# Building one tile's weights on ScalarE and VectorE instead of TensorE, at the start of a fused mixture-convolution and quantised feed-forward kernel

## The reference

```python
agg_w = jnp.einsum('bk,koi->boi', att, weight[..., 0])
y = jnp.einsum('boi,bih->boh', agg_w, x) + agg_b[:, :, None]
qg, sg = quant(y * inv_gate); qu, su = quant(y * inv_up)      # round(v / scale), scale = max|v| / 127
gate = (qg @ w_gate.T) * sg * s_wgate; up = (qu @ w_up.T) * su * s_wup
inter = clip(silu(gate) * up, -10, 10)
qi, si = quant(inter * inv_inter)
out = x + (qi @ w_down.T) * si * s_wdown
```

## Time and profile before

| | |
|---|---|
| median of 3 runs | 804.18 us (804.02 to 804.37) |
| profiled execution | 804.37 us, of which the span from first to last instruction is 802.6 us |
| TensorE busy | 793.7 us, 99% |
| VectorE busy | 716.2 us, 89% |
| ScalarE busy | 441.0 us, 55% |
| GpSimd busy | 146.1 us, 18% |

### The profile page before, as it was taken

The page is one execution under the profiler, slowest core; times in us unless marked ns, Lnnn a source line. Parts: engine busy times, 40 slices in busy tenths (PEclk is TensorE's granted clock), DMA queues, the critical chain, the costliest instruction groups (busy, mean ns, idle before and its releaser), DMA issues.

```text
span 802.6 us, 9187 instructions
## 1 busy us (share of the span) xinstructions
PE 793.7 (99%) x3521; PEld 365.1 (45%) x3521; DVE 716.2 (89%) x810; ACT 441.0 (55%) x385; POOL 146.1 (18%) x138
## 2 busy tenths in 40 slices
PE   8999999999999999999999999999999999999997
PEld 4554444444444444444444444444444444444443
DVE  6987899999888998888998888998888988888968
ACT  6774335556664545654555654555654546655531
POOL 2603210210122220122220222210222210222000
PEclk9999999999999999999999999999999999999999
DMA  9997745554445444445444455445455544354342
GB/s 298 241 216 154 163 135 179 146 170 124 127 145 171 145 145 123 120 151 169 146 145 118 118 158 164 150 145 111 120 163 159 156 136 128 107 168 153 94 108 105
DMA packets 162964, 119.81 MB, mean 149 GB/s; under 512 B 151780, under 2 KB 152164, under 8 KB 153703
## 3 DMA queue, kind: packets, MB, share of 16 engines
q1 hardware_dynamic: 161192, 106.64, 44.7%
q0 software_dynamic: 1728, 12.58, 7.7%
HBM read 60.48 MB, written 33.55 MB: 117 GB/s over the span
## 4 chain that ended last, share of the span: by engine, by line
PE 91%; DVE 6%; ACT 2%; issue 1%; DMA 0%; DVEq 0%; ACTq 0%
PE gate_ps L614 26%; PE up_ps L614 26%; PE down_ps L717 23%; PE conv_ps L567 12%; DVE amax L1093 1%; PE gate_ps L717 1%; ACT y L810 0%; DVE region L1165 0%; PE down_ps L572 0%; DVE down_sc L1257 0%; DVE xt L1266 0%; DVE part_max L1172 0%; PE conv_ps L572 0%; ACT wd L810 0%; DVE region L1111 0%
## 5 line engine op out<-in xcount | busy, mean ns | idle before, releaser
L717 PE MATMUL down_ps<-wd,qiT 128*128 128x512 bf16 x896 | 211.2, 379 | 0.0
L614 PE MATMUL gate_ps<-wg,qgT 128*128 128x512 bf16 x928 | 205.7, 379 | 0.0
L614 PE MATMUL up_ps<-wu,quT 128*128 128x512 bf16 x896 | 202.4, 379 | 0.0
L1093 DVE TENSOR_REDUCE amax<-region 128x1 f32<-128x2048 f32 (+1 forms) x90 | 173.1, 1923 | 1.2
L442 POOL TENSOR_TENSOR prod<-wexp,att_bc 128x1024 f32<-128x1024 f32 x28 | 53.1, 1896 | 540.2 <-DVE region L1151 498.5
L717 PEld LDWEIGHTS down_ps<-wd,qiT 128*128 128x128 bf16 x896 | 87.5, 98 | 123.4 <-issue 29.1
L614 PEld LDWEIGHTS gate_ps<-wg,qgT 128*128 128x128 bf16 x928 | 90.7, 98 | 109.5 <-issue 1.1
L614 PEld LDWEIGHTS up_ps<-wu,quT 128*128 128x128 bf16 x896 | 87.7, 98 | 106.1 <-ACT quT L886 0.4
L821 ACT ACTIVATE qg<-region,recip 128x2048 f16<-128x2048 f32 x30 | 60.1, 2002 | 128.3 <-DVE recip L1103 128.3
L567 PE MATMUL conv_ps<-xt,aggw 128*128 128x512 f32 x244 | 116.3, 599 | 1.4 <-ACT y L810 0.8
L810 ACT ACTIVATE y<-conv_ps,aggb 128x512 bf16<-128x512 f32 x116 | 78.9, 686 | 60.0 <-PE conv_ps L567 55.4
(11 more groups left out here) (180 smaller groups left out, 581.2 us busy)
## 6 DMA issues: line engine op xcount, KB each, us to landing
xt<-x SPq DMA_DIRECT2D x30, 1024.0 KB, 4.8
out<-xt SPq DMA_DIRECT2D x29, 1024.0 KB, 4.0
wg<-w_gateT POOLq DMA_DIRECT2D x4, 1024.0 KB, 20.5
wu<-w_upT POOLq DMA_DIRECT2D x4, 1024.0 KB, 17.2
wd<-w_downT POOLq DMA_DIRECT2D x4, 1024.0 KB, 8.6
xt<-x SPq DMA_DIRECT2D x4, 512.0 KB, 4.7
invg_bc<-inv_gate SPq DMA_DIRECT2D x1, 1024.0 KB, 8.7
out<-xt SPq DMA_DIRECT2D x2, 512.0 KB, 2.9
```

The costliest lines, as they stand in the source:

```text
L614: last = nc.tensor.matmul(acc[:, n * BANK:(n + 1) * BANK], codes[:, k * P:(k + 1) * P], wts[:, k, n * BANK:(n + 1) * BANK], start=(k == 0) ...
L717: last = nc.tensor.matmul(down_bank(t, c), qiT_at(t)[:, k * P:(k + 1) * P], wd[:, k, c * BANK:(c + 1) * BANK], start=(k == ks[0]), stop=(k ...
L1093: nc.vector.tensor_reduce(amax[:, i:i + 1], src, axis=AX.X, op=ALU.max, apply_absolute_value=True).then_inc(max_ready, 1)
```

## The change

Tile 2's experts are multiplied by eight ScalarE products into a free part of wu (`prod2`) and added up by three VectorE sums in place of TensorE's eight products; the division by the softmax sum moves into ScalarE's writing of y. The sums stand in VectorE's list after the second quarter of tile 0. Tile 3's diagonal blocks are made by GpSimd (L465's product, now for tile 3 and ahead of the weights), no longer by VectorE. TensorE does convolutions 0, 1 and 2 in one go, and convolution 3 where convolution 2 was. Tile 3's y has a home of its own (quT), so that it waits for less. The gate weights' transfers wait for input 1 instead of input 0, and input 3 is issued without waiting. The orders of ScalarE and VectorE are changed accordingly: VectorE does gate 1, gate 2, up 0, up 1 instead of gate 1, up 0, gate 2, up 1. GpSimd issues the up weights only when the sums are done.

```diff
-        Y_HOME = [y[:, :], wd_part(0, bf16), wd_part(1, bf16)]
+        Y_HOME = [y[:, :], wd_part(0, bf16), wd_part(1, bf16), quT[:, :]]
...
+        prod2 = wu[:, 4:6, :].rearrange("p k i -> p (k i)").bitcast(fp32).rearrange("p (k o) -> p k o", o=P)
...
-            sp.wait_ge(wg_in[0], 16)
             sp.dma_start(xslot(3), x[3, :, :]).then_inc(x_in[3], 16)
...
-            pool.wait_ge(x_in[0], 16)
+            pool.wait_ge(att_dve, BIAS[0])
+            a = att_bc[:, EARLY * K:FIRST * K].unsqueeze(2).to_broadcast([P, K, P])
+            nc.gpsimd.tensor_tensor(diag_at[EARLY].rearrange("p (k r) -> p k r", r=P),
+                                    ident[:, :].unsqueeze(1).to_broadcast([P, K, P]), a, ALU.mult).then_inc(diag_pool, 1)
+            pool.wait_ge(x_in[1], 16)
             for i in range(WCH):
                 load(wg, w_gateT, i, wg_in)
-            pool.wait_ge(exp_done, 1)
-            pool.wait_ge(agg_mm, 1)
-            a = att_bc[:, 2 * K:3 * K].unsqueeze(2).to_broadcast([P, K, P])
-            nc.gpsimd.tensor_tensor(diag_at[2]...).then_inc(diag_pool, 1)
             pool.wait_ge(rows_in[0], 16)
             spread(invu_bc[:, :], rows_s[:, 0:2 * I])
...
+            pool.wait_ge(sum2, 3)
             for i in range(WCH - 1):
                 load(wu, w_upT, i, wu_in)
...
             conv(0)
             conv(1)
-            aggregate_mm(2)
+            conv(2)
             turn_g(0, range(1))
-            aggregate_mm(3)
+            aggregate_mm(EARLY)
             gate(0, range(4))
             turn_g(0, range(1, 2))
-            conv(2)
+            conv(EARLY)
             turn_g(1)
             gate(0, range(4, 8))
             gate(1, HALVES[0])
-            conv(3)
...
+            def experts2(ks):
+                for k in ks:
+                    nc.scalar.activation(prod2[:, k, :], wexp[:, k, :], ACT.Copy, scale=att_col(2, k)).then_inc(scaled2, 1)
...
+                elif t == 2:
+                    act.wait_ge(xu_ready, FIRST)
...
-            conv_out(0)
+            experts2(range(4))
+            conv_out(0, range(1))
+            experts2(range(4, 6))
+            conv_out(0, range(1, 2))
+            experts2(range(6, 7))
+            conv_out(0, range(2, NC))
+            experts2(range(7, K))
             conv_out(1)
+            conv_out(2, range(1))
             quant_g_first(0)
-            aggregate_out(2)
+            conv_out(2, range(1, 2))
+            quant_g_first(1)
             turned_g(0, range(1))
-            quant_g_first(1)
-            aggregate_out(3)
+            aggregate_out(EARLY)
+            conv_out(2, range(2, NC))
             turned_g(0, range(1, 2))
             quant_g(1)
-            conv_out(2, range(2))
-            turned_g(1, range(1))
-            conv_out(2, range(2, NC))
-            turned_g(1, range(1, 2))
+            conv_out(EARLY)
+            turned_g(1)
+            quant_g(2)
             quant_u(0)
-            conv_out(3)
-            quant_g(2)
             turned_g(2)
...
+            def experts2_sum():
+                dve.wait_ge(scaled2, K)
+                nc.vector.tensor_tensor(prod2[:, 0:4, :], prod2[:, 0:4, :], prod2[:, 4:8, :], ALU.add).then_inc(sum2, 1)
+                dve.wait_ge(sum2, 1)
+                nc.vector.tensor_tensor(prod2[:, 0:2, :], prod2[:, 0:2, :], prod2[:, 2:4, :], ALU.add).then_inc(sum2, 1)
+                dve.wait_ge(sum2, 2)
+                nc.vector.tensor_tensor(aggw2, prod2[:, 0, :], prod2[:, 1, :], ALU.add).then_inc(sum2, 1)
...
+                    if c == 1:
+                        experts2_sum()
...
             quant_first()
-            diagonals(3)
             quant_g(1)
+            quant_g(2)
             quant_u(0)
-            quant_g(2)
             quant_u(1)
             xg_product(3)
             gate_out(0)
```

More of the change, by code:

```diff
@@ L92, in y_at @@
         def y_at(t):
-            return Y_HOME[t] if t < EARLY else y[:, :]
+            return Y_HOME[t] if t <= EARLY else y[:, :]
         def xg_at(t):
@@ L145, in adaln_ffn @@
         ones = qiT[:, 0:2 * P].bitcast(fp32)
+        aggw2 = qiT[:, 4 * P:6 * P].bitcast(fp32)
         filler = region1[:, 0:(P + BANK) // 2].bitcast(bf16)
@@ L159, in adaln_ffn @@
         SPLIT = 5
-        diag_at = [region2[:, I:H], prod_flat, region2[:, I:H], prod_flat]
+        diag_at = {0: region2[:, I:H], EARLY: region2[:, I:H]}
+        prod2 = wu[:, 4:6, :].rearrange("p k i -> p (k i)").bitcast(fp32).rearrange("p (k o) -> p k o", o=P)
         def diag_part(t, k):
@@ L245, in adaln_ffn @@
         diag_act = sem("diag_act")
-        diag_dve = sem("diag_dve")
+        scaled2 = sem("scaled2")
+        sum2 = sem("sum2")
         diag_pool = sem("diag_pool")
@@ L300, in conv_bank @@
         def conv_bank(t, c):
-            return bank(up_ps, c - 2) if t < EARLY and c >= 2 else bank(conv_ps, c % 2)
+            return bank(up_ps, c - 2) if t <= EARLY and c >= 2 else bank(conv_ps, c % 2)
         def down_bank(t, c):
@@ L309, in last_half, with aggw_at @@
             return bank(up_ps if h else down_ps, 1 - h)[:, 0:BANK // 2]
+        def aggw_at(t):
+            return aggw2 if t == 2 else aggw[t % 2][:, :]
         def xcols(t, c):
@@ L530, in aggregate_mm @@
                     pe.wait_ge(wexp_in, 16)
-                elif t == 2:
+                else:
                     pe.wait_ge(diag_pool, 1)
-                else:
-                    pe.wait_ge(diag_dve, 1)
                 for k in ks:
@@ L550, in conv @@
                         pe.wait_ge(agg_sum, 1)
-                    elif t < POOLED:
-                        pe.wait_ge(agg_out, t - 1)
+                    elif t == 2:
+                        pe.wait_ge(sum2, 3)
+                    elif t == EARLY:
+                        pe.wait_ge(agg_out, 1)
                     else:
@@ L560, in conv @@
                             pe.wait_ge(logits_out, 1)
-                    elif t < EARLY or (t == EARLY and c < 2):
+                    elif t <= EARLY:
                         pe.wait_ge(y_ready, NC * t + c - 3)
@@ L585, in turn_g @@
                         pe.wait_ge(gcodes_ready, 1)
-                        pe.wait_ge(agg_out, 2)
+                        pe.wait_ge(agg_out, 1)
                     turn(gturn_ps[:, h * I:(h + 1) * I], qg, KI, h * KI, gturn_mm)
@@ L623, in gate @@
                         pe.wait_ge(qgT_ready, t - EARLY)
[L624 to L627, removed]
+                    if t == 1:
+                        pe.wait_ge(y_ready, NC * FIRST)
                     elif t == 2 or t == EARLY:
@@ L840, in aggregate_out @@
             def aggregate_out(t):
-                act.wait_ge(agg_mm, t)
-                act.wait_ge(conv_done, NC * (t - 1))
+                act.wait_ge(agg_mm, 2)
+                act.wait_ge(conv_done, NC * 2)
                 nc.scalar.activation(aggw[t % 2][:, :], agg_ps[t], ACT.Copy, scale=erec[:, t:t + 1]).then_inc(agg_out, 1)
```

17 lines of the change are left out of this document (3 added, 14 removed).

## The result

| kernel | executions | median, us | lowest to highest | ratio to before, 95% interval |
|---|---|---|---|---|
| before, beside it | 7 | 804.18 | 804.01 to 804.37 | |
| after | 7 | 806.28 | 805.75 to 807.88 | 1.0031 [1.0021, 1.0041] |

A forecast was written before the change was run, and what follows sets the result against it. VectorE, not TensorE, was to set tile 2's gate start: 46.4 us undisturbed, plus 0.7 for a broadcast collision, 47.1 against 47.20. That 0.1 off gave 804.3 for the profiled execution, 804.2 median; range 803.0 to 806.5.

The forecast's parts named there:

- The start: When TensorE begins tile 2's gate product, 47.20 us in before, was said to decide the end.
- The wait on region2: VectorE's up 1 product waits for ScalarE to write up 0's codes from the shared buffer: 2.1 us idle.
- input 1: Freed of the gate weights' competition, its transfer was to land at 13.75 us in place of 14.4.
- GpSimd's diagonal product: GpSimd's product for tile 3 was to run from about 9.9 to 11.8 us, ending a 0.9 us VectorE wait.
- the order of the prediction: VectorE's product for tile 2's gate starts (25.73 us) before GpSimd's first broadcast, which waits until 28.0.
- the second collision: The second broadcast was to hold up VectorE's product of up 0 by 0.7 us.
- GpSimd's six broadcasts: Step placing the first broadcast at 25.1 to 26.4 us, where broadcasts and VectorE's two-SBUF-operand products shut each other out.
- I take this one: Choice of VectorE's gate 2 product before broadcast 1: tile 2's gate at 47.1 us, median 804.2, chance 0.40.
- The early case: Rival: first broadcast just ahead of gate 2's product, tile 2's gate at 48.7, 805.7 to 806.3 us; chance 0.34.
- no reload: Rival: the 8.7 us before the first broadcast were the rows' transfer; broadcasts start at 16.6, 807.5 us; chance 0.08.
- A fall to half speed is taken as nothing and would come on top: TensorE's clock falling after idling before tile 2's gate was given no time in the forecast.
- From there on the code is the same: Behind tile 2's gate start both kernels were said to match but for two homes of data.

The follow-up runs named there:

- e9_again_third: The kernel after, unchanged, run once more on a third chip; median 804.74 us, 1.0016 of before.
- e2_sched: The kernel after with the first broadcast held until VectorE's tile 2 gate product is done and the others until up 0's product; median 804.99 us.
- e10_fill: The kernel after with eight matmuls of 384 columns, results unread, on TensorE ahead of tile 2's gate product; median 805.59 us, 1.0014 of before.
- e5_again: The kernel after, unchanged, run again in the second set on another chip; median 804.25 us, profiled execution 807.76 us.
- e4_hold: The kernel after with the gate weights' transfers waiting for input 0 again instead of input 1; median 804.97 us, 1.0014 of before.
- e11_home_pad_vector: e7_home_early_quarter with eight one-column memsets more at the head of VectorE's program; median 802.69 us, 0.9982 of before.
- e7_home_early_quarter: The kernel after with tile 1's up product in a fourth home and the up weights' second quarter issued ahead of the broadcasts; median 803.05 us.
- e12_home_pad_tensor: e7_home_early_quarter with eight matmuls of 16 columns more at the head of TensorE's program; median 802.86 us, 0.9984 of before.
- e1_home: The kernel after with tile 1's scaled up product in the fourth home, so it no longer waits for region2; median 803.82 us.

## Why the prediction was wrong

**Bound and price of the parts: right.** The start settles the matter but for 0.38 us, and VectorE, not TensorE, sets it. The wait on region2 measured 2.07 (forecast 2.1); input 1, the convolutions in one go and GpSimd's diagonal product (9.93, forecast 9.9) came as worked out. In e9_again_third, which has the order of the prediction, the product of tile 2 starts at 25.57 (25.73). Its gate starts at 46.45, where 47.1 was forecast: the second collision cost 0.43 (2.72 for 2.29), not 0.7, and the rest of the chain was quicker. That 803.99 still lies near the 804.3 forecast for such an execution is luck in part: the gate was put 0.65 too late, and 0.38 behind it was missed. TensorE was ready later than the 44.85 forecast: 45.28 there (46.45 - 1.17), 45.92 in after, where the first four passes of convolution 0 took 3.75 against 2.76. The granted clock reads 1.00 over these passes in both, so what lengthened them is not shown.

**The step that failed is the choice under "GpSimd's six broadcasts"**: "I take this one", the product first. Its reason was a stretch of 10 us ahead of the first broadcast; in the three profiled executions of after it was 9.19, 9.38 and 9.98, and over those of the whole family 9.10 to 10.94 (e2_sched, which holds the broadcast, left out). The start window given there, 25.1 to 26.4, holds these three (25.21, 25.49, 25.96), not e10_fill (27.19). Where the broadcast falls is drawn anew in each execution, and so is the product's place (25.54 to 26.59), which goes with the length of those first passes (2.68 to 3.75). With the product first by 0.39 us the time was 804.0; with the broadcast first by 0.33 tile 2's gate started 2.07 later. The two cases had nearly equal chances in the prediction (0.40 and 0.34), which is about what 29 executions show (12 against 17). But a median goes wholly to one side, and the first seven all lay on the other; whether by chance or by the chip is open. The early case's parts hold: product held by 1.7 (1.68 in e5_again), up 0's by 0.6 (0.58: 2.87 for 2.29). Its time too (805.7 to 806.3; 805.75, median 806.28), but partly by luck: the gate was put at 48.7 and came at 48.24 and 48.52, and 0.38 was lost behind it. In after the product was held by 0.74 only, as it began at 26.49. The rival "no reload" is out: the broadcast came over 9 us behind the last issue in every profiled execution of the family. One slip of arithmetic changes nothing: 0.1 off the median of 804.18 is 804.1, not 804.2.

The Trainium skill, SBUF — State Buffer, section Who interferes with whom, says that the later of two such instructions is blocked until the first is done. The rows agree nearly: in e5_again and in after the product ends 2.00 and 2.01 us behind the broadcast's end (29.79 - 27.79, 29.52 - 27.51), 0.29 less than its full 2.29.

**Taken as nothing, wrongly: the clock.** "A fall to half speed is taken as nothing and would come on top": it was 1.69 us in e5_again, and came in 7 of 29 executions. After 2.32 us without work the clock stayed in after, after 3.06 it fell in e5_again, but after 1.89 it fell in e4_hold: the length of the wait alone does not tell. The Trainium skill, TensorE: Matmul & The Clock Gate, section What's actually happening, has the array halved when it idles and released by activity; the rows above agree.

**Not seen at all: 0.38 us behind the gate.** "From there on the code is the same" is true of the code, not of how much stands ahead of it. It is not the two homes of data either: e11_home_pad_vector has both and has lost the 0.38. It lifts even the best case: 46.45 is 0.75 ahead of 47.20, and 803.99 only 0.38 ahead of 804.37.

**Sum of the first set's median:** gate 1.04 later in the profiled execution and 0.34 behind it make 1.38 (805.75 - 804.37). The other six have no trace, but their granted clock is on record: 0.997 and 0.998 in the three at 807.43 to 807.88, which thus had the fall (1.69), and 0.999 or more in the three at 806.15 to 806.28. What is left over 805.75 is 0.0 to 0.5 us. In after and e5 the gate started 23.03 behind the broadcast (48.24 - 25.21, 48.52 - 25.49), so by these rows a broadcast at 25.2 to 25.7 covers it; that is an estimate.

**What beats both kernels:** e11_home_pad_vector, 802.69 us, 0.9982 [0.9973, 0.9991] of before. It keeps the change, moves one tile's product to a free home (ends the 2.07 us wait), issues one quarter of the up weights ahead of the broadcasts (the first broadcast comes too late for the race) and pads VectorE's program. Its medians do not part it from e7_home_early_quarter and e12_home_pad_tensor; only the profiled executions do. Of the 33 executions of the three none is over 803.93.

## What to carry to other kernels

When a change frees one engine, look at the order of writes on the next: a wait of 2.07 us on a reused buffer appeared because the product that had lain between two others was moved. When two instructions that shut each other out come within some tenths of a microsecond of each other, and one of them stands behind a stretch whose length varies by 1.8 us, forecast two times and not one; and rather than guess, move one of them clear, as one early transfer did here. Idle time opened ahead of a matmul is to be priced twice: as itself, and as the clock that may fall in it.

## What the runs showed of the hardware

- From GpSimd's last weight issue to the same first broadcast it took 9.10 to 10.94 us in twelve profiled executions (8.72 in the earlier trace rows). No row names what fills it. It runs on its own: in e2_sched, where the broadcast was held until VectorE's product ended at 28.36, it started at 28.61. The Trainium skill, GPSIMD Engine Reference, section Instruction dispatch, gives some 6 us for loading the code of a first call; no run here was that short.
- One VectorE instruction, the same in every tile, waited 0.36 us longer in the last but one tile, in every profiled execution of the family but e11_home_pad_vector's; there eight instructions more at the head of its program took that away.
- In e1_home's profiled execution TensorE waited 20.87 us for a quarter of the down weights, issued at 69.27 and later while a transposing transfer of tile 3's codes was under way. Both crawled: from 84 to 104 us all queues moved 63 GB/s. The same two overlap in e11_home_pad_vector (transposing transfer issued at 66.43, quarter at 69.35), which took 802.50 us. What starts it is open; it was not tried.
